# Spectral mixer: in the layers of nine slots, the call of the last transform placed behind the column transform instead of in front of it

## What is computed

```python
xs = jnp.fft.rfft2(xf32, axes=(1, 2))          # per channel, over rows and columns
xs = xs.reshape(B, H, Wm, 8, 48)               # 8 blocks of 48 channels
o1r = relu(xr @ w1[0] - xi @ w1[1] + b1[0])    # complex two-layer MLP inside a block
o1i = relu(xi @ w1[0] + xr @ w1[1] + b1[1])
o2r = o1r @ w2[0] - o1i @ w2[1] + b2[0]
o2i = o1i @ w2[0] + o1r @ w2[1] + b2[1]
out = irfft2(softshrink(o2r) + 1j * softshrink(o2i)) + x
```

## Time and profile before

| | |
|---|---|
| median of 3 runs | 2077.69 us (2076.89 to 2084.58) |
| the profiled execution: its time, its span | 2080.81 us, 2079.0 us |
| busy share of the span: PE, PEld | 93%, 76% |
| busy share of the span: DVE, ACT, POOL | 57%, 49%, 21% |
| granted TensorE clock, mean | 0.976 |
| layer 0, about | 18 to 350 us |
| layer 1 and token MLP, about | 350 to 1466 us |
| layers 2 and 3, about | 1466 to 2079 us |

### The profile page before, as it was taken

How to read it: one execution, slowest core, us unless ns; L and a number is a source line. 1 busy time by engine, 2 the same in 40 slices (tenths; PEclk the granted TensorE clock), 3 DMA queues, 4 the chain that set the end, 5 groups by cost and what they waited for, 6 DMA issues and landing times.

```text
span 2079.0 us, 68971 instructions
## 1 busy us (share of the span) xinstructions
PE 1934.2 (93%) x31104; PEld 1581.3 (76%) x31104; DVE 1175.1 (57%) x2480; ACT 1011.0 (49%) x1644; POOL 434.7 (21%) x425
## 2 busy tenths in 40 slices
PE   5999995698998999999999999999899999999997
PEld 4777672576776999999999999999677777777774
DVE  3687887987855433333333333332467667666675
ACT  3766545576753333333333333333466556655652
POOL 3212103975721000000000000000321121211200
PEclk9999996799998999999999999999999999999998
DMA  9424728307444111111111111114813555457214
GB/s 169 92 49 84 128 58 140 59 8 125 117 103 98 31 31 31 31 30 30 30 30 30 30 30 30 30 31 73 130 16 68 91 101 103 70 86 127 60 36 95
DMA packets 299701, 141.05 MB, mean 68 GB/s; under 512 B 275760, under 2 KB 298032, under 8 KB 299440
## 3 DMA queue, kind: packets, MB, share of 16 engines
q1 hardware_dynamic: 299440, 137.08, 35.9%
HBM read 74.14 MB, written 62.91 MB: 66 GB/s over the span
## 4 chain that ended last, share of the span: by engine, by line
PE 81%; DVE 9%; ACT 3%; issue 2%; POOL 2%; DMA 2%; SPq 1%; DVEq 0%; POOLq 0%; ACTq 0%
PE ps L690 19%; PE ps L675 19%; PE ps L523 9%; PE ps L586 8%; PE ps L537 8%; PE ps L602 7%; PE ps L555 5%; PE ps L504 4%; DVE u L934 3%; DVE st L971 2%; PE ps L565 1%; DVE xs L959 1%; PE ps L660 1%; ACT zf L749 1%; POOL xs L1180 1%
## 5 line engine op out<-in xcount | busy, mean ns | idle before, releaser
L1083 DVE TENSOR_TENSOR gl<-g,gh 128x512 fp32r<-128x512 f32 x192 | 156.8, 817 | 476.4 <-ACT gh L869 476.4
L934 DVE TENSOR_TENSOR u<-ps,clamp 64x192 f32<-64x192 f32 (+1 forms) x864 | 377.0, 436 | 27.7
L866 ACT ACTIVATE g<-ps,colp 128x512 f32<-128x512 f32 x192 | 132.3, 689 | 529.4 <-PE ps L675 529.4
L523 PEld LDWEIGHTS ps<-const,z 128*48 128x48 f32 x8384 | 266.6, 124 | 117.2 <-issue 107.2
L729 ACT ACTIVATE z<-ps 64x512 f32<-64x512 f32 x366 | 234.6, 641 | 113.4 <-PE ps L504 106.6
L523 PE MATMUL ps<-const,z 128*48 128x64 f32 (+1 forms) x8384 | 271.5, 217 | 14.0 <-issue 9.0
L1170 POOL COPY xn<-xs 128x512 f32<-128x512 f32 x144 | 151.2, 1088 | 552.7 <-PE ps L504 364.3
L690 PE MATMUL ps<-w2h,gh 128*128 128x384 f32 x768 | 261.8, 341 | 0.0
L690 PE MATMUL ps<-w2h,gl 128*128 128x384 f32 x768 | 258.5, 337 | 0.0
L690 PE MATMUL ps<-w2l,gh 128*128 128x384 f32 x768 | 257.5, 335 | 0.0
L537 PE MATMUL ps<-zf,w 112*64 112x512 f32 (+2 forms) x992 | 248.3, 574 | 5.9 <-ACT zf L749 1.3
(11 more groups left out here) (70 smaller groups left out, 2516.2 us busy)
## 6 DMA issues: line engine op xcount, KB each, us to landing
after<-xs SPq DMA_DIRECT2D x96, 384.0 KB, 5.4
xs<-after SPq DMA_DIRECT2D x94, 384.0 KB, 8.9
after<-om SPq DMA_DIRECT2D x32, 384.0 KB, 4.3
out<-xs SPq DMA_DIRECT2D x32, 384.0 KB, 5.4
xm<-after SPq DMA_DIRECT2D x30, 384.0 KB, 6.3
xs<-in_x SPq DMA_DIRECT2D x24, 384.0 KB, 8.4
wstage<-in_spectral SPq DMA_DIRECT2D x16, 210.0 KB, 5.7
xs<-in_x SPq DMA_DIRECT2D x4, 768.0 KB, 11.9
```

The source lines that it names most:

```text
L523: mm = pe.matmul(ps[a * SIDE:a * SIDE + BLOCK, F2_BANK, n * L.kh:(n + 1) * L.kh], z[:, g % 2, slot, :], basis(col + a * SIDE, L.kh), start ...
L934: dve.tensor_tensor(u[to, g % 2, :, start + b:start + size:BATCH], whole, limited, ALU.subtract).then_inc(u_ready, 1)
L1083: dve.tensor_tensor(gl[:, n % 4, :], g[:, n % 2, :], gh[:, n % 4, :], ALU.subtract).then_inc(g_low, 1)
```

## The change

In the loop over slots, for the layers of nine slots, all `f6` calls of a slot now stand behind `f2` and in front of `f1`, `f5` and `m2`. For layer 1 the order stays as it was. Nothing else differs: no instruction is added or removed, and the orders of the other engines are the same.

```diff
-                        for r in rows[0:1]:
-                            f6(*r)
+                        if not L.full:
+                            for r in rows[0:1]:
+                                f6(*r)
                         f2(g, t)
                         if L.full:
+                            for r in rows:
+                                f6(*r)
                             for k in ahead:
                                 f1(g + 1, k)
                         for k in behind[0:1]:
                             f5(g - 1, k)
-                        for r in rows[1:]:
-                            f6(*r)
                         if not L.full:
+                            for r in rows[1:]:
+                                f6(*r)
                             for k in ahead:
                                 f1(g + 1, k)
```

## The result

| | before | changed |
|---|---|---|
| median of 6 runs, us | 2078.95 (2076.89 to 2084.58) | 2060.94 (2058.25 to 2069.37) |
| profiled execution: time, span, us | 2080.81, 2079.0 | 2058.86, 2057.0 |

The ratio is 0.9914, with a 95% interval of 0.9896 to 0.9931. So the change takes off 18 us, 0.86%. The forecast was 10.1 us with an end of the range at 2062.0: the direction was right, the size too small, and the measured time lies outside the range.

A forecast was written before the change was run, and what follows sets the result against it. TensorE, busy 1934.2 of 2079.0 us, was taken as the bound, so only its pauses could change. Layers 2 and 3 (8.0 us) plus layer 0 (2.1) gave 10.1 us: 2077.7 to 2067.6 us, range 2062 to 2076.

The forecast's parts named there:

- The signs named for it: Waits of m1 for zf fall from 44 to a few; a group takes 34.7 us; group 7 keeps a saturated VectorE.
- the terms of a full group: Pauses removed in slots 8, 0 and 1 of layers 2 and 3: 0.21 + 0.10 + 0.23 = 0.54 us a group.
- Slot 8: zf ends earlier, so the pause between m2 and m1 goes: 0.76 - 0.55 = 0.21 us a full group.
- Slot 0: f6 comes 0.67 us later while VectorE's addition keeps its place, so its pause of 0.10 us goes.
- Slot 1: zf starts earlier behind a late h; of m1's pause of 0.30 us, 0.23 us goes.
- 0.07 stays: In slot 1, m1 could start at 1690.52 against a free place of 1690.45, so 0.07 us of pause remains.
- layer 0: Groups 2, 4 and 6 gain 1.6 us, slot 8 of group 1 0.2, groups 3, 5 and 7 0.3: 2.1 us.
- 0.3 was set for three groups: Layer 0's groups 3, 5 and 7, held by VectorE's pace through statistics, gain 0.3 us together.
- won and given back: Rival: instruction supply sets TensorE's pace, so time won only lengthens its pauses; 2073 to 2078, say 2075 us; chance 0.14.
- A dearer handover: Rival: f6's first weight load isn't hidden behind f2; 162 moved calls at 0.15 us cost 24.3 us, 2091.9 us; chance 0.06.
- Given back later: The rival that time won is lost again at TensorE's instruction supply; say 2075 us, chance 0.14.
- all stages use nearly all rows: On TensorE, every entry to a stage would show its weight load; entries don't differ, so the sum stays unchanged.

The follow-up runs named there:

- slots801: Against the changed kernel, f6 stands behind f2 only in slots 8, 0 and 1, elsewhere in front as before; 2062.5 us, ratio 0.9917.
- slots2to6: Against the changed kernel, f6 stands behind f2 only in slots 2 to 6, elsewhere in front as before; 2081.5 us, ratio 1.0000.
- slot8: Against the changed kernel, f6 stands behind f2 only in slot 8, elsewhere in front as before; 2081.5 us in a single profile.
- cheap_after: The changed kernel with layer 0's statistics instructions reading 8 channels instead of 96, so results are not those asked for; 2053.4 us in one run.

## Why the prediction was wrong

**Right: the place and the mechanism.** Pauses of `m1` for `zf` in slots 8 and 1, and of `f6` for the addition in slot 0, were what the order took away. slots801 and slots2to6 show it, and the steps of the table name the same slots. The signs named for it came: `zf` waits fell from 44 to 3, and group 7 still has a saturated VectorE, busy 45.21 of 48.00 us (268 to 316 us).

**Wrong: the size of the terms of a full group, 0.54 us against 0.72 to 0.80.**
- *Slot 8, 0.21 forecast, 0.26 measured.* The free distance from `m2` to `m1` was read behind `f1`, 0.55 us. Behind `f6` it is 0.50.
- *Slot 0, 0.10 forecast, 0.15 measured.* The late start of the next `f2`, 0.05 us, was seen and left out.
- *Slot 1, 0.23 forecast, 0.27 and 0.04 measured.* The step "0.07 stays" failed. I let `zf` start behind the recorded end of `h`. It doesn't wait so long:

```profile
1679.95 0.58 ACT L775 ACTIVATE h<-ps,w 113x384 f32<-113x384 f32 x1
1680.43 0.59 ACT L752 ACTIVATE zf<-ps 112x512 f32<-112x512 f32 x1
```

`h` ends at 1680.53 by its row, and `zf` starts at 1680.43. So it is in all 20 places of the changed kernel where `zf` with 512 columns follows an `h` with 384 at once. It is no rule for all activations: one `z` behind another starts 0.02 us after the recorded end. The 0.04 us are the restart of `m1`, which I hadn't counted.

Over 14 full groups and the rest of layers 2 and 3 this is about 11 us where 8.0 were forecast. The slot 8 term had a second fault that the full change hides: it holds only if `f6` moves in slot 0 as well, as the run slot8 shows.

**Right, in part by luck: layer 0.** 2.1 us forecast, 2.4 by the three profiles each, which scatter by 0.8 and 1.6 us among themselves. Groups 3 and 5 gained 0.13 and 0.19 us in the first profile, where 0.3 was set for three groups, and cheap_after shows why it isn't more.

**Wrong: the issue pauses were taken only as a loss.** The rival "won and given back" had them swallow the gain, and the range gave them 2 us. They are 5 us less in the changed kernel; why is not shown. A forecast couldn't have told their sign from one trace, but their sum was there to be read, and the range should have been wider by some 5 us on both sides. With the larger terms alone the time would have been near 2064 us (2077.7 - 11 - 2.4), inside the range; it is the pauses that put it outside.

**The rivals.** A dearer handover: not there, slots2to6 has the periods of before. Given back later: it happens where slot 8 is moved alone, at VectorE's addition and not at the supply. One reading beside them was wrong: that all stages use nearly all rows and that entries don't differ. The row transform works on 64 rows (64x64), and it is just the entry to it that costs 0.10 us more than the others.

## What to carry to other kernels

Where one engine is busy 93% of the time, look for the slots of its schedule that lack a filler between a product and the product that reads its copy; a call moved into them cost nothing here and paid up to 0.27 us each time. Read the free distance behind the neighbour that the new order will have, and try moves together that free the same queue: one alone may only shift the wait. In a long program, leave room for the issue pauses: here a change of order shifted them by 5 us, beside an effect of its own of some 13.

## What the runs showed of the hardware

- In layers 2 and 3, TensorE's pauses without a semaphore stand at whole multiples of 256 of its own instructions, at 12 of 105 such ends in before. Over the whole span such pauses sum to 26 to 37 us in the twenty profiles. In the three profiles of before most begin while the DMA engines are busy (30 of 36), with paced loads they don't (1 of 7).
- Behind the pause of 3.09 us the granted clock was 0.53 in the next stretch of 2 us, and the group took about 2 us more. Behind one of 2.44 us it stayed at 1.00.
- `zf` starts 0.10 us before the recorded end of an `h` with 384 columns when it need not wait (20 of 20), a `z` behind another `z` 0.02 us after it.
- The entries `f2` to `f6` (0.67 and 0.89 us) and `f6` to `f5` (0.65 us) cost nothing beyond the work, and `f6` to `f1` 0.75 us, so the entry to `f1` costs 0.10 us whatever stands ahead of it.
